# Two of nine value taps move from VectorE to GpSimd, and key maps are built with 13 columns a block

## What is computed

```python
kv = jnp.einsum('oc,bchw->bohw', qkv_w, x)
kv = _dw3x3(kv, qkv_conv_w)                   # depthwise, nine taps a channel
k, v = jnp.split(kv, 2, axis=1)
q = _ssl(x, conv5_w, conv7_w, conv9_w)        # wavelet analysis, 3x3 taps, synthesis
q = q / jnp.maximum(jnp.linalg.norm(q, axis=-1, keepdims=True), eps)
k = k / jnp.maximum(jnp.linalg.norm(k, axis=-1, keepdims=True), eps)
attn = jax.nn.softmax(jnp.einsum('bhdn,bhen->bhde', q, k) * temperature, axis=-1)
out = jnp.einsum('bhde,bhen->bhdn', attn, v).reshape(b, c, h, w)
```

## Time and profile before

| | |
|---|---|
| median of three runs | 1417.45 us (1417.22 to 1420.52) |
| the profiled execution | 1423.73 us, of it 1422.1 us span |
| mean granted TensorE clock | 0.929 |
| busy share of the span | TensorE 83%, VectorE 77%, ScalarE 57%, GpSimd 16% |
| taps on VectorE (L942) | 448 into PSUM, 64 into SBUF, 808 and 799 ns each |
| GpSimd's low_x (L735) | 32, 3105 ns each |

### The profile page before, as it was taken

One profiled execution on the slowest core, in us unless ns is written; L12 is line 12 of the kernel. 1 busy time (PEld: TensorE's weight loads), 2 busy tenths in 40 slices (PEclk: granted clock), 3 DMA queues, 4 the chain that ended last, 5 costly groups with the idle time before them and its releaser, 6 DMA issues. The chain is left out here.

```text
span 1422.1 us, 36051 instructions
## 1 busy us (share of the span) xinstructions
PE 1186.1 (83%) x12648; PEld 933.7 (66%) x12648; DVE 1095.2 (77%) x1929; ACT 808.5 (57%) x1414; POOL 231.8 (16%) x241
## 2 busy tenths in 40 slices
PE   0899928899999899998999999954999997999900
PEld 0555527789989899897998989842555554555500
DVE  6777617989999899999999999914777776063394
ACT  0677735666766667666676666501444444766383
POOL 6100021213132131321313213011100001000000
PEclk9999967989999899999999999975999999999955
DMA  9966693343444434444344443115677743000079
GB/s 333 415 282 267 279 205 87 88 125 89 125 137 98 131 90 125 128 103 134 90 125 131 104 129 89 55 61 234 233 266 273 239 131 138 0 1 1 0 274 407
DMA packets 148844, 221.23 MB, mean 156 GB/s; under 512 B 115768, under 2 KB 116932, under 8 KB 144336
## 3 DMA queue, kind: packets, MB, share of 16 engines
q1 hardware_dynamic: 137600, 152.26, 35.1%
q0 software_dynamic: 6480, 47.19, 8.8%
q10 hardware_dynamic: 4608, 19.67, 4.0%
HBM read 131.85 MB, written 87.20 MB: 154 GB/s over the span
## 5 line engine op out<-in xcount | busy, mean ns | idle before, releaser
L942 DVE SCALAR_TENSOR_TENSOR b_value_sum<-b_vin,b_vtaps,b_value_sum 128x576 f32<-128x576 f32 x448 | 362.1, 808 | 3.5 <-ACT b_value_sum L868 2.9
L1653 PE MATMUL b_conv_bank<-b_sign,wsign 128*128 (+1 forms) x1728 | 299.7, 328 | 7.7 <-ACT b_sign L1451 7.5
L1653 PEld LDWEIGHTS b_conv_bank<-b_sign,wsign 128*128 128x128 bf16 x1728 | 167.9, 97 | 144.7 <-issue 30.9
L984 PE MATMUL b_bank<-b_yh,b_tmh 96*96 96x200 f16 x768 | 200.6, 261 | 51.2 <-DVE b_feat L949 23.5
L896 ACT CAST b_feat<-b_bank 96x400 f16<-96x400 f32 x255 | 124.8, 489 | 199.1 <-PE b_bank L986 196.7
L984 PE MATMUL b_bank<-b_tkh,b_kt 96*96 96x100 f16 x1536 | 229.0, 214 | 2.4 <-DVE b_tml L965 2.2
L985 PE MATMUL b_bank<-b_tkl,b_kt 96*96 96x100 f16 x1536 | 227.8, 213 | 0.0
L986 PE MATMUL b_bank<-b_tkh,b_kt 96*96 96x100 f16 x1536 | 227.8, 213 | 0.0
L984 PEld LDWEIGHTS b_bank<-b_tkh,b_kt 96*96 96x96 f16 x1536 | 198.6, 129 | 4.8 <-DVE b_tml L965 2.5
L986 PEld LDWEIGHTS b_bank<-b_tkh,b_kt 96*96 96x96 f16 x1536 | 198.6, 129 | 0.0
L985 PEld LDWEIGHTS b_bank<-b_tkl,b_kt 96*96 96x96 f16 x1536 | 197.2, 128 | 0.0
(11 more groups left out here) (230 smaller groups left out, 2332.6 us busy)
## 6 DMA issues: line engine op xcount, KB each, us to landing
b_vin<-value_projection_scratch SPq DMA_DIRECT2D x32, 686.0 KB, 5.1
keys_scratch<-b_khl SPq DMA_DIRECT2D x24, 784.0 KB, 3.4
value_projection_scratch<-b_vout ACTq DMA_DIRECT2D x24, 784.0 KB, 4.7
b_kt<-keys_scratch SPq DMA_DIRECT2D x128, 147.0 KB, 2.9
b_xraw<-in_x SPq DMA_DIRECT2D x128, 144.0 KB, 4.9
values_scratch<-b_vacc SPq DMA_DIRECT2D x32, 576.0 KB, 3.2
values<-values_scratch SPq DMA_DIRECT2D x48, 384.0 KB, 3.7
out<-xs SPq DMA_DIRECT2D x25, 576.0 KB, 6.8
```

What stands on the lines that cost most here:

```text
L942: nc.vector.scalar_tensor_tensor(whole if t == 8 else part, src, vtaps[:, t:t + 1], part, ALU.mult, ALU.add).then_inc(s_tap, 1)
L984: nc.tensor.matmul(out, w_hi, m_hi, start=first, stop=False)
L1653: ins = nc.tensor.matmul(cbank[k % NBK][:, 0:CH].rearrange("p (r c) -> p r c", c=W), p["wsign"][nth // NIMG][:, t * C:(t + 1) * C], padded ...
```

## The change

GpSimd takes taps 7 and 8, VectorE keeps 1 to 6, ScalarE keeps tap 0. VectorE's last tap is now the sixth and writes to `vacc`; `TAP_AT` has 12 places. GpSimd makes the product of a whole slab (128x1152) with one tap's weight in a new SBUF tensor `vprod` and adds it to `vacc` in place, twice: the first product once the slab is there (`first_product`, at the end of its group), the rest (`finish_slab`: add, product, add) at the start of the next group, behind VectorE's last tap. The store waits for the second add. `edges` moves ahead of `low_x`, because its scratch `eprod` is now a part of `vprod`. `KT` becomes 13: still 8 blocks, but 12 x 13 columns each, and tables of 117 rows; this makes `tk` narrower.

```diff
-KT, KPB = 14, 3
+KT, KPB = 13, 3
...
-        eprod = sb("b2_eprod", [W, 4, 2, NIMG * HD * 2])
+        vprod = sb("b2_product", [C, SLAB * W])
+        eprod = vprod[0:W, 0:8 * NIMG * HD * 2].rearrange("p (a s n) -> p a s n", a=4, s=2)
...
-        TAP_AT = (0, 1, 2, 3, 5, 6, 7, 8, 10, 11, 12, 13, 15, 16, 17, 18)
+        DVE_TAPS = (1, 2, 3, 4, 5, 6)
+        POOL_TAPS = (7, 8)
+        NTAP = 2 * len(DVE_TAPS)
+        PSTEPS = 2 * len(POOL_TAPS)
+        TAP_AT = (0, 2, 3, 5, 7, 8, 10, 12, 13, 15, 17, 18)
...
-                sp.wait_ge(s_tap, i * 16 + 16)
+                sp.wait_ge(s_ptap, i * PSTEPS + PSTEPS)
...
+            def product(slot, t):
+
+                nc.gpsimd.tensor_tensor(vprod[:].rearrange("p (r c) -> p r c", c=W),
+                                        vin[:, slot, :].rearrange("p (r c) -> p r c", c=WP)[:, t // 3:t // 3 + SLAB, t % 3:t % 3 + W],
+                                        vtaps[:, t:t + 1].unsqueeze(2).broadcast_to([C, SLAB, W]), ALU.mult).then_inc(s_ptap, 1)
+
+            def add_product(slot):
+                nc.gpsimd.tensor_tensor(vacc[:, slot, :], vacc[:, slot, :], vprod[:], ALU.add).then_inc(s_ptap, 1)
+
+            def first_product(i, slot):
+
+                pool.wait_ge(s_seed, i * 2 + 1)
+                pool.sem_inc(s_carry, 1)
+                product(slot, POOL_TAPS[0])
+
+            def finish_slab(i, slot):
+
+                pool.wait_ge(s_tap, i * NTAP + NTAP)
...
+                add_product(slot)
...
+                product(slot, POOL_TAPS[1])
...
+                add_product(slot)
...
-            def body(k, i, how):
+            def body(k, i, how, head=None):
+                if k:
+                    finish_slab(i - 1, (k - 1) % 2)
+                if how != LAST and not (isinstance(i, int) and i + 2 >= NG):
+                    pool.wait_ge(s_pe, i * J + LEAD)
+                    pool.sem_inc(s_carry, 1)
+                    spread_taps(i + 2, k % 2)
+                if head is not None:
+                    edges(head, k // GPH % 2 ^ 1, i)
                 if how != LAST:
-                    if not (isinstance(i, int) and i + 2 >= NG):
-                        pool.wait_ge(s_pe, i * J + LEAD)
-                        pool.sem_inc(s_carry, 1)
-                        spread_taps(i + 2, k % 2)
                     low_x(i + 1, (k + 1) % 2)
+                first_product(i, k % 2)
...
-                nc.vector.scalar_tensor_tensor(whole if t == 8 else part, src, vtaps[:, t:t + 1], part,
+                nc.vector.scalar_tensor_tensor(whole if t == DVE_TAPS[-1] else part, src, vtaps[:, t:t + 1], part,
                                                ALU.mult, ALU.add).then_inc(s_tap, 1)
```

More of the change, by code:

```diff
@@ L581, in block_grams @@
         s_tap = sem("b2_value_tap_added")
+        s_ptap = sem("b2_value_pool_tap_step")
         s_vst = [sem(f"b2_value_slab_stored{k}") for k in range(2)]
@@ L772, in null_parts @@
                 nc.gpsimd.tensor_tensor(enull, ends[:, :, :, 0], ends[:, :, :, 1], ALU.add).then_inc(s_edge, 1)
-            def body(k, i, how):
+            def product(slot, t):
[11 more added lines that the diff above has]
+                pool.sem_inc(s_carry, 1)
+                pool.wait_ge(s_ptap, i * PSTEPS + 1)
+                pool.sem_inc(s_carry, 1)
+                add_product(slot)
+                pool.wait_ge(s_ptap, i * PSTEPS + 2)
+                pool.sem_inc(s_carry, 1)
+                product(slot, POOL_TAPS[1])
+                pool.wait_ge(s_ptap, i * PSTEPS + 3)
+                pool.sem_inc(s_carry, 1)
+                add_product(slot)
+                pool.wait_ge(s_ptap, i * PSTEPS + 4)
+                pool.sem_inc(s_carry, 1)
+            def body(k, i, how, head=None):
[3 more added lines that the diff above has]
+                    pool.wait_ge(s_pe, i * J + LEAD)
+                    pool.sem_inc(s_carry, 1)
+                    spread_taps(i + 2, k % 2)
+                if head is not None:
+                    edges(head, k // GPH % 2 ^ 1, i)
                 if how != LAST:
-                    if not (isinstance(i, int) and i + 2 >= NG):
-                        pool.wait_ge(s_pe, i * J + LEAD)
-                        pool.sem_inc(s_carry, 1)
-                        spread_taps(i + 2, k % 2)
                     low_x(i + 1, (k + 1) % 2)
+                first_product(i, k % 2)
             def edges(head, parity, i):
@@ L788, in edges @@
                 null_parts(head, parity)
+                pool.wait_ge(s_edge, head + 1)
+                pool.sem_inc(s_carry, 1)
             pool.wait_ge(s_c, 7 * 16)
@@ L797, in _ @@
                 for k in range(PAIR):
-                    i = hh * PAIR + (PEEL + k)
-                    body(PEEL + k, i, MID)
-                    if k % GPH == 0:
-                        edges(hh * 2 + k // GPH, k // GPH, i)
+                    body(PEEL + k, hh * PAIR + (PEEL + k), MID, hh * 2 + k // GPH if k % GPH == 0 else None)
             for i in range(NG - GPH, NG):
-                body(i, i, LAST if i + 1 == NG else MID)
-                if i == NG - GPH:
-                    edges(HEADS - 2, (HEADS - 2) % 2, i)
+                body(i, i, LAST if i + 1 == NG else MID, HEADS - 2 if i == NG - GPH else None)
+            finish_slab(NG - 1, (NG - 1) % 2)
             pool.wait_ge(s_dve, TAIL + 1)
@@ L935, in tap @@
                 part = vsum[:, :, 0:HALF // 2 * W].rearrange("p b (r c) -> p b r c", c=W)
-                if t == 1:
+                if t == DVE_TAPS[0]:
                     dve.wait_ge(s_seed, i * 2 + (half + 1))
                 else:
-                    dve.wait_ge(s_tap, i * 16 + m)
-                if m == 7:
+                    dve.wait_ge(s_tap, i * NTAP + m)
+                if m == len(DVE_TAPS) - 1:
                     dve.wait_ge(s_vst[slot], loads * 16)
-                nc.vector.scalar_tensor_tensor(whole if t == 8 else part, src, vtaps[:, t:t + 1], part,
+                nc.vector.scalar_tensor_tensor(whole if t == DVE_TAPS[-1] else part, src, vtaps[:, t:t + 1], part,
                                                ALU.mult, ALU.add).then_inc(s_tap, 1)
@@ L959, in body @@
                         m += 1
-                assert m == 16, m
+                assert m == NTAP, m
             for m, (kind, j) in enumerate(lead):
```

4 lines of the change are left out of this document (2 added, 2 removed).

## The result

| | before | after |
|---|---|---|
| median | 1418.99 us (1417.22 to 1425.12) | 1372.88 us (1371.18 to 1374.79) |
| ratio | | 0.9677, 95% interval 0.9657 to 0.9697 |
| the profiled execution | 1423.73 us | 1372.45 us, of it 1370.8 us span |
| first to last low_x | 696.0 us | 647.0 us |
| a head of four undisturbed groups | 87.0 us | 81.4 us |

What follows compares the result with a forecast made beforehand. VectorE was taken to bound the second stage, TensorE next. Gains of 38.8 + 6.6 + 2.0 + 1.5 less 2 make 46.9 us: 1423.73 to 1376.8, less 6.3 for the median, 1370.5 us; range 1352 to 1400.

Steps and rivals of the forecast that it cites:

- VectorE's need of 18.76 us: Second stage, per group: four taps at 0.72 us and 0.1 us of narrower key blocks off 21.74 us.
- TensorE next, 81.1 us a head: Second stage: TensorE becomes the later engine in three groups of four; a head falls from 87.0 to 81.1 us.
- GpSimd: Second stage: four new instructions a group, 9.3 to 10.3 us, fit beside the path; later low_x costs nothing, at worst 1 us a head.
- SyncE's queue: Store 8 to 9 us later; image rows' load just fits before normalise; otherwise up to 1 us a head.
- 24 undisturbed intervals: Second-stage low_x intervals of 21.7 to 21.8 us: three first, 14 second or third, seven without Gram work gain 38.8 us.
- three with the clock down: Intervals with lowered clock after a group without Gram work: TensorE idles less, 2.2 us gained each, 6.6 in all.
- four at the start and the jumps: Intervals at the stage's start and loop jumps, TensorE already the bound: 0.5 us gained each, 2.0 in all.
- end of the stage: Last Gram stores wait behind GpSimd's chain, so ScalarE's copy slips: costs 2 us, range 0.5 to 3.
- TensorE as full as its busy time: Rival, chance 0.16: a head can't fall under 81.93 us, waits keep it at 83 to 84; 1383 to 1398 us.
- ScalarE's normalise as VectorE's wait: Rival, chance 0.10: normalise's 2.51 us fall out of every group, VectorE needs 21.3 us; about 1408 us.
- GpSimd the bound: Rival, chance 0.06: at 4.09 us an instruction a head needs 90.2 us, kernel slower, 1444 us.
- A shared port: Rival, chance 0.02: GpSimd's new instructions stop VectorE, 27 us more a head, about 1627 us.

Runs made afterwards that it cites:

- the cut: Changed kernel with 12 of 36 matmuls of every kg job left out: 1348.71 us, ratio 0.9499; the same edit in the kernel before: 1420.87 us.
- the new places of the Gram matmuls: Changed kernel with a head's 100 Gram matmuls spread in pieces of 9 and 8 over all four groups, none added or removed: 1362.77 us, ratio 0.9602.
- the kernel with the stores moved: Changed kernel with head 6's Gram stores ahead of the last slab's store in SyncE's queue: 1370.20 us, ratio 0.9659.

## Why the prediction was right, step by step

**VectorE as the bound.** Right. Less work for TensorE gave nothing before the change; a tenth of a microsecond on VectorE moved the interval by 0.09.

**VectorE's need of 18.76 us.** Nearly right. Where VectorE is close to full behind the change (the cut), it is busy for 75.67/4 = 18.92 us a group; the forecast for the head was 75.04. An instruction that waits shows its whole duration and not its distance (0.81 and 0.73 us for a tap), so each wait adds a little.

**TensorE next, 81.1 us a head.** Right, 81.41, and both the cut (81.4 to 77.6) and the new places of the Gram matmuls (81.4 to 79.6) show that TensorE's load per group sets it. The four single intervals, 21.2, 20.2, 20.2 and 19.5, can't be read from low_x: its start lies in the middle of a group and moves with GpSimd's chain. They can be read on TensorE, from its first product with b_xl in one group to that in the next:

```profile
297.95:318.07 20.12, 20.02 (x320) 19.49 (x319) 19.45 (x33) 14.34 (x28) 18.55 (x17) 1.00 0.47 126
318.07:338.61 20.54, 20.01 (x319) 19.44 (x318) 18.90 (x33) 15.13 (x29) 14.16 (x8) 1.00 0.55 124
338.61:359.52 20.91, 20.91 (x329) 20.48 (x328) 19.02 (x32) 14.88 (x28) 14.40 (x8) 1.00 0.46 121
359.52:379.35 19.83, 18.32 (x321) 17.47 (x320) 19.18 (x33) 14.58 (x30) 12.44 (x8) 1.00 0.50 129
```

TensorE is nearly full in three groups, and in the fourth VectorE is (19.18 of 19.83), as forecast. But the order was wrong: I gave a head's Gram matmuls as 40, 30, 30 and 0, and in the traces of both kernels these groups hold 30, 30, 40 and 0. In that order the forecast is 20.2, 20.2, 21.2 and 19.5. The head's sum stays the same; the sum over the 24 undisturbed intervals doesn't, since only three first groups are among them and seven third ones: 15.4 + 3.8 + 13.4 + 2.2 = 34.8 and not 38.8. The slip made the forecast gain 4 us too large.

**GpSimd.** The product at 2.3 us measured 2.11, the add at 2.3 to 2.9 measured 2.64, the chain at 7.5 to 8.6 measured 7.7. A low_x that starts later at no cost: shown, 81.41 with and 81.40 without, though it is 2.7 us later in the groups with edges and not 1 to 2. The step that was too kind is the point from which GpSimd decides. I put it at 87 us, the old head. That is where the kernel gets slower than before, but the gain shrinks from the new head of 81.1 on: by the same working from 3.5 us an instruction and not 3.9. With three taps GpSimd's own 84.2 us are above it, and its place in front of low_x makes TensorE wait.

**SyncE's queue.** "Just fits" held. In the group with edges the rows' load is issued until 562.61 and needs 4.8 us, and the normalise of these rows starts at 569.07: 1.7 us to spare.

```profile
560.32 2.29 SPq L670 DMA_DIRECT2D b_xraw<-in_x  x4
...
569.07 2.51 ACT L891 ACTIVATE b_xraw<-b_xraw,row_stats 96x384 f32<-96x384 f32 x4
```

**The sum by terms.** The 31 intervals of low_x in the two profiled executions, in their order, the seven disturbed ones taken out by their number (of before: 1, 2, 4, 5, 13, 21 and 29). The 24 others add up to 521.82 and 485.47 us, the three with the clock down (4, 5 and 29) to 72.0 and 63.8, the four at the start and the jumps to 102.2 and 97.7:

| term | forecast | measured |
|---|---|---|
| 24 undisturbed intervals | 38.8 | 36.4 |
| three with the clock down | 6.6 (1.5 to 13.5) | 8.1 |
| four at the start and the jumps | 2.0 (0 to 6) | 4.5 |
| last group | 1.5 (0 to 2.9) | 4.0 |
| end of the stage | -2 (-3 to -0.5) | -3.8 |
| together | 46.9 | 49.2 |

The first three terms can be compared only together, 47.4 forecast and 49.0 measured. In the changed kernel the late low_x moves 2.7 us from a head's second interval to its first, and two such firsts (5 and 29) stand in the second term while their seconds stand in the first. With taps 7 and 8 left out, where this shift is absent, the 24 gain 31.2 and not 36.4. That 36.4 lies near 38.8 is therefore luck.

The last two terms lie outside their ranges and cancel. The end's cost was under-sized because I counted the late copy and not the lower clock behind the standstill that it brings; what the last group gained is worked out from the kernel with the stores moved (47.5 us from the last low_x to the last copy before, 43.5 there). The other 2 us of the 51.3 between the profiled executions lie outside these terms, 1.5 of them before the stage's first low_x (206.1 and 204.6).

**The base.** Between the medians lie 46.1 us, between the profiled executions 51.3: the profiled one of before was 4.7 us above its median, the one of after 0.4 below. Subtracting the 6.3 us was only half right as a step, since the sum takes 6.6 us from the three intervals with the clock down, and such intervals come and go between executions. In the profiled execution of the narrower key builds alone (1417.10 us) the fourth and fifth interval are 21.71 and 21.65 us, where before has 24.02 and 23.92. How many of them before's median execution had, no trace shows. That the forecast came within 2.4 us is in part luck: this step and the order of the Gram matmuls made the gain too large, and the terms at the start, the jumps and the last group were too small.

**The rivals.** *TensorE as full as its busy time*: no, 81.41 is below the 81.93 that were said to be the least, and the busy time itself fell to 79.26 with the same matmuls. *ScalarE's normalise as VectorE's wait*: it is there, 0.57 us a group and not 2.5, and costs 0.75 us a head. *GpSimd the bound*: not with two taps, but with three. *A shared port*: no. The Trainium skill's Perfetto Trace Analysis, Optimizing Scalar/DVE Operations, warns that moving work between these two engines might not help; here it did. Taps of 806 ns beside a busy GpSimd agree with what the Trainium skill's SBUF — State Buffer, Who interferes with whom, says of VectorE instructions with one SBUF input. No run here tests one with two.
